# A routed feed-forward kernel: tiles of one expert instead of two, projections made once per token and gathered

## What is computed

```
g = base_g + x @ gate_A[e] @ gate_B[e] * 0.25     # gate_A: 256 x 64, gate_B: 64 x 896
u = base_u + x @ up_A[e]   @ up_B[e]   * 0.25
h = silu(g) * u                                    # 896 wide
oe = h @ base_down + h @ down_A[e] @ down_B[e] * 0.25
out = out + routing[e] * oe                        # routing: softmax of the two bids
```

## Time and profile before

| | |
|---|---|
| median of three runs | 350.17 us (349.76 to 350.34) |
| span of the profiled execution | 343.0 us (the page gives no other time of it) |
| TensorE matmul busy | 262.8 us, 77% |
| VectorE (DVE) busy | 220.6 us, 64% |
| ScalarE (ACT) busy | 160.7 us, 47% |
| GpSimd (POOL) busy | 129.1 us, 38% |
| memory traffic | 133 GB/s over the span |

### The profile page before, as it was taken

How to read it: one execution, slowest core, us unless ns; L and a number is a source line. 1 busy time by engine, 2 the same in 40 slices (tenths; PEclk the granted TensorE clock), 3 DMA queues, 4 the chain that set the end, 5 groups by cost and what they waited for, 6 DMA issues and landing times.

```text
span 343.0 us, 5103 instructions
## 1 busy us (share of the span) xinstructions
PE 262.8 (77%) x1500; PEld 229.4 (67%) x1501; DVE 220.6 (64%) x433; ACT 160.7 (47%) x277; POOL 129.1 (38%) x148
## 2 busy tenths in 40 slices
PE   3474363537278899995999999999999999998600
PEld 2251241214167799994999999999999999997500
DVE  2979975798952881006666777777777777775325
ACT  0443875196336363343455555555555555555211
POOL 3528376537441441109233333333333333311121
PEclk9996566555579899998999999999999999999965
DMA  7803333013663646446244444434344444420065
GB/s 259 240 23 80 70 84 84 26 51 107 177 158 134 210 167 267 175 164 214 44 139 139 139 138 133 143 135 141 134 138 142 138 136 138 140 106 15 15 193 190
DMA packets 30189, 45.67 MB, mean 133 GB/s; under 512 B 13976, under 2 KB 25632, under 8 KB 30176
## 3 DMA queue, kind: packets, MB, share of 16 engines
q0 software_dynamic: 4416, 21.50, 18.9%
q1 hardware_dynamic: 20752, 14.03, 14.6%
q10 hardware_dynamic: 5008, 9.98, 7.9%
HBM read 33.57 MB, written 11.93 MB: 133 GB/s over the span
## 4 chain that ended last, share of the span: by engine, by line
PE 65%; DVE 17%; issue 5%; DMA 4%; POOL 3%; ACT 3%; SPq 1%; DVEq 0%; ACTq 0%; POOLq 0%
PE pY L55 8%; PE pY L59 7%; PE pY L57 7%; PE pG L55 5%; PE pT L1395 5%; PE pG L59 4%; PE pG L57 4%; PE pU L57 4%; PE pU L55 4%; PE pU L59 4%; DMA x_resid<-in_x_dram 2%; DVE q L899 2%; DMA yr<-results 1%; DVE q L819 1%; DVE am L821 1%
## 5 line engine op out<-in xcount | busy, mean ns | idle before, releaser
L496 POOL DMA_INDIRECT results<-yb,dest x19 | 19.0, 998 | 91.9 <-DVE yb L1108 91.9
L55 PE MATMUL pY<-Wd_hi,hT_hi 128*128 128x384 f32 x133 | 47.5, 357 | 0.9 <-ACT Wd_lo L694 0.8
L59 PE MATMUL pY<-Wd_hi,hT_lo 128*128 128x384 f32 x133 | 44.7, 336 | 0.0
L57 PE MATMUL pY<-Wd_lo,hT_hi 128*128 128x384 f32 x133 | 44.6, 336 | 0.0
L490 POOL DMA_INDIRECT bin<-base_products,tok x18 | 22.0, 1221 | 24.8 <-PE pU L59 15.2
L704 ACT CAST hT_hi<-pT 128x896 fp32r<-128x896 f32 x19 | 17.2, 907 | 24.1 <-PE pT L1395 24.1
L680 ACT CAST xaT_hi<-pX 128x256 fp32r<-128x256 f32 x19 | 7.1, 373 | 42.5 <-PE pX L1372 42.0
L55 PEld LDWEIGHTS pY<-Wd_hi,hT_hi 128*128 128x128 f32 x133 | 25.0, 188 | 2.3 <-DVE hT_lo L1096 1.0
L57 PEld LDWEIGHTS pY<-Wd_lo,hT_hi 128*128 128x128 f32 x133 | 25.1, 188 | 0.0
L482 POOL DMA_INDIRECT xin<-normed,tok x19 | 18.6, 979 | 16.9 <-PE pX L1358 9.9
L59 PEld LDWEIGHTS pY<-Wd_hi,hT_lo 128*128 128x128 f32 x133 | 25.0, 188 | 0.0
(11 more groups left out here) (260 smaller groups left out, 742.2 us busy)
## 6 DMA issues: line engine op xcount, KB each, us to landing
base_products<-brow ACTq DMA_DIRECT2D x8, 896.0 KB, 3.9
yr<-results SPq DMA_DIRECT2D x8, 256.0 KB, 4.6
raw<-in_L_ffn_gate_B_dram SPq DMA_DIRECT2D x8, 224.0 KB, 2.7
raw<-in_L_ffn_up_B_dram SPq DMA_DIRECT2D x8, 224.0 KB, 2.5
raw<-in_L_ffn_down_A_dram SPq DMA_DIRECT2D x7, 256.0 KB, 3.0
x_resid<-in_x_dram SPq DMA_DIRECT2D x4, 256.0 KB, 4.8
q<-in_fside_BxS2xS_dram ACTq DMA_DIRECT2D x4, 256.0 KB, 5.7
normed<-q ACTq DMA_DIRECT2D x4, 256.0 KB, 2.8
```

Of the source, the lines that this page charges most:

```text
L55: m.matmul(outs[i], hi, whi[i], start=first, stop=False, skip_group_check=True)
L57: m.matmul(outs[i], hi, wlo[i], start=False, stop=False, skip_group_check=True)
L59: ins = m.matmul(outs[i], lo, whi[i], start=False, stop=last, skip_group_check=True)
L496: g.indirect_dma_start(out=yg, out_offset=bass.IndirectOffsetOnAxis(ap=dest[:, j:j + 1], axis=0), in_=yb[:, :], in_offset=None).then_inc(d ...
```

## The change

A group is one expert (`GE = 1`): 8 groups, so at most 23 tiles instead of 19. The projections x @ gate_A and x @ up_A are made ahead of the loop, for every token and all eight experts, scaled by 0.25 and written to a new tensor in memory (`projected`, a row of 128 values for each token and expert); a tile gathers its 128 rows of it instead of rows of x. A gathered row holds 64 values for gate and 64 for up, so after one transpose gate lies on partitions 0 to 63 and up on 64 to 127. The B matrices lie the same way. The expert's B is copied by ACT into a fixed place for each tile (`stage_B`), and its `down_A` one tile ahead (`stage_dA`). No masks are left. Tile 0 gathers its base rows like the others. PSUM has two banks for the result (`pY[2]`), and the transposes of z and of the projections share a bank with half of `h_T`.

```
-GE = 2
+GE = 1
...
+    xa_rows = nc.dram_tensor("projected", [NB * S * E, P], F32, kind="Internal").ap()
...
+        pZ, pX = pT[:, 1, 0:P], pT[:, 1, P:2 * P]
...
             lo(CH_1 - lo_done[0])
+            pool.wait_ge(s_made, 2 * NT)
+            lo(CH_2 - CH_1)
             def gather(j):
-                if j:
-                    pool.wait_ge(s_xT, j)
+                if j >= 2:
+                    pool.wait_ge(s_xzT, j - 1)
+                g.indirect_dma_start(out=xin[:, j % 2, :], out_offset=None, in_=xa_rows, ...
...
             pool.wait_ge(s_plan, 1)
             pool.wait_ge(s_share, 3)
+            pool.wait_ge(s_made, ITEMS)
+            for i in range(3):
+                pool.wait_ge(d_bn[i], 16 * ITEMS // 3)
+            for j in range(2):
+                gather(j)
+                gather_base(j)
+            lo(NCH - CH_2)
+            for j in range(2, PT + 3):
+                if j < PT:
                     gather(j)
                     gather_base(j)
                 if j >= 3:
                     scatter(j - 3)
```

ACT (base products and projections are items; kind 2 is a projection of 1024 columns):

```
+            def item_out(n):
+                t, kind = item(n)
+                act.wait_ge(s_made, n + 1)
...
+                a.activation(row.rearrange("p (a i) -> p a i", a=2), pp[:, :, 0:w], ACT.Copy,
+                             scale=(1.0, 1.0, SCALING)[kind]).then_inc(s_copied, 1)
+                act.wait_ge(s_copied, n + 1)
...
+                a.dma_start(to, row).then_inc(d_bn[n % 3], 16)
...
+            def tile(j, first=False, ahead=2):
+                h_hi(j, 0, first)
+                h_hi(j, 1, first)
+                e = expert(j + 2) if ahead == 2 else None
+                if ahead == 2:
+                    stage_B(j + 2, 0, e)            # waits s_exp: expand(j+1) done
+                if ahead >= 1:
+                    silu(j + 1)
+                xz_hi_copy(j, not first, ahead == 2)  # waits s_xzT: z_T(j-1) and xa_T(j+2) done
+                if ahead == 2:
+                    stage_B(j + 2, 1, e)
+                if ahead >= 1:
+                    e = expert(j + 1)
+                    stage_dA(j + 1, 0, e)           # waits s_down: down_products(j) done
+                    stage_dA(j + 1, 1, e)
```

DVE:

```
+            def tile(j, par, first=False, second=False, ahead=2):
+                if not first:
+                    z_copy(j - 1, 1 - par, second)
+                h_lo(j, 0)
+                h_lo(j, 1)
+                if ahead >= 1:
+                    g_add(j + 1, 1 - par)
+                    u_add(j + 1, 1 - par)
+                if not first:
+                    z_lo(j - 1)
+                if ahead == 2:
+                    xa_lo(j + 2)
+                if ahead >= 1:
+                    h_mul(j + 1)
+                if not first:
+                    y_copy(j - 1, 1 - par, second)
```

PE:

```
+            for t in range(4, NT):
                 base(t)
+            for t in range(NT):
+                products(2 * NT + t)
+            pe.wait_ge(s_copied, ITEMS)
...
+            def expand(j):
+                pe.wait_ge(s_xalo, j + 1)
+                pe.wait_ge(s_WBe, 2 * (j + 1))
...
+                for i in range(2):
+                    cols = slice(i * IH, (i + 1) * IH)
+                    for k, (x_, w_) in enumerate(((xaT_hi, WBe_hi), (xaT_hi, WBe_lo), (xaT_lo, WBe_hi))):
+                        m.matmul(pG[:, i, 0:IH], x_[0:R, :], w_[0:R, cols], start=(k == 0), stop=(k == 2))
+                        ins = m.matmul(pU[:, i, 0:IH], x_[R:P, :], w_[R:P, cols], start=(k == 0), stop=(k == 2))
+                ins.then_inc(s_exp, 1)
...
+            def tile(j, par, first=False, ahead=2):
+                h_T(j, ahead == 0)          # two halves, 4 and 3 transposes
+                if ahead >= 1:
+                    expand(j + 1)
+                down_products(j, par, range(0, 4))
+                pe.wait_ge(s_hlo, 2 * j + 2)
+                if not first:
+                    ins = z_T(j - 1)
+                if ahead == 2:
+                    ins = xa_T(j + 2, par)      # waits d_xin: gather(j+2) landed
+                ins.then_inc(s_xzT, 1)
+                down_products(j, par, range(4, IC))
+                if not first:
+                    down_B_products(j - 1, 1 - par, expert(j - 1))
```

More of the change, by code:

```diff
@@ L657, in _ @@
             a.activation(share[:, 1, :], dif[:, :], ACT.Sigmoid, scale=-1.0).then_inc(s_share, 1)
[L658 removed]
+            for t in range(3, NT):
                 split(3)
@@ L751, in _ @@
+            tile(PT - 1, ahead=0)
+            xz_hi_copy(PT, xa=False)
             for b in range(0, NB, 2):
@@ L1107, in y_copy @@
                     dve.wait_ge(d_y, 16 * j)
-                v.tensor_copy(yb[:, :], pY[:, 0:H]).then_inc(s_yc, 1)
-            def tile(j, slot, back2=True, back3=True, last=False):
-                if back2:
-                    z_lo(j - 2)
-                h_lo(j - 1)
-                if back2:
-                    y_copy(j - 2, not back3)
-                g_add(j, slot)
-                if not last:
-                    x_lo(j + 1)
-                u_add(j, slot)
-                h_mul(j)
-                if not last:
-                    xa_mask(j + 1)
-                    xa_lo(j + 1)
-                z_mask(j - 1, not back2)
@@ L1136, in _ @@
+            xa_lo(0)
+            g_add(0, 0)
+            u_add(0, 0)
             xa_lo(1)
             h_mul(0)
-            tile(1, 1, back2=False)
-            tile(2, 0, back3=False)
-            tile(3, 1)
-            with dve.Fori(4, PT - 2, 2) as j:
+            tile(0, 0, first=True)
+            tile(1, 1, second=True)
+            with dve.Fori(2, PT - 3, 2) as j:
                 tile(j, 0)
                 tile(j + 1, 1)
-            tile(PT - 1, (PT - 1) % 2, last=True)
-            z_lo(PT - 2)
@@ new lines, in h_T @@
+            def h_T(j, last=False):
+                pe.wait_ge(s_h, j + 1)
+                if not (isinstance(j, int) and j == 0):
+                    pe.wait_ge(s_hlo, 2 * j)
+                for half, chunks_ in enumerate((range(0, 4), range(4, IC))):
+                    if half and not last:
+                        pe.wait_ge(s_xalo, j + 2)
+                    if half and not (isinstance(j, int) and j < 2):
+                        pe.wait_ge(s_zlo, j - 1)
+                    for c in chunks_:
+                        ins = m.transpose(pT[:, half, (c % 4) * P:(c % 4 + 1) * P], hbuf[:, c * P:(c + 1) * P], ident[:, :])
+                    ins.then_inc(s_hT, 1)
@@ L1461, in _ @@
-            expand_B(0, 0, (0, 1), e, first=True)
-            project_A(1, group(1))
-            expand_B(0, 1, (0, 1), e, True)
-            xa_T(1)
-            h_T(0, True)
-            tile(1, back2=False)
-            tile(2)
-            tile(3)
-            with pe.Fori(4, PT - 2, 2) as j:
-                tile(j)
-                tile(j + 1)
-            tile(PT - 1, last=True)
-            z_T(PT - 2)
-            down_B_products(PT - 2, group(PT - 2))
-            down_products(PT - 1, range(IC))
@@ L1481 @@
+            xa_T(0, 0).then_inc(s_xzT, 1)
+            expand(0)
+            xa_T(1, 1).then_inc(s_xzT, 1)
+            tile(0, 0, first=True)
+            tile(1, 1)
+            with pe.Fori(2, PT - 3, 2) as j:
+                tile(j, 0)
+                tile(j + 1, 1)
+            tile(PT - 3, 0)
+            tile(PT - 2, 1, ahead=1)
+            tile(PT - 1, 0, ahead=0)
+            z_T(PT - 1).then_inc(s_xzT, 1)
+            down_B_products(PT - 1, 0, expert(PT - 1))
 _INS = ['x', 'fside_BxS2xS2_0', 'ctx_1024', 'g_xattn', 'g_ffn', 'L0_ffn_expert_wealth', 'L0_ffn_conf_W', 'L0_ffn_conf_b',
```

527 lines of the change are left out of this document (205 added, 322 removed).

## The result

The changed kernel takes 368.25 us, median of three runs (366.35 to 369.57), against 350.17: 1.050 times the time before, 95% interval 1.044 to 1.056. It is slower, by 18.1 us where 21.8 were forecast (372). The profiled execution took 366.35 us with a span of 364.6, 21.6 more than the span of before; the forecast had +22.1.

What follows compares the result with a forecast made beforehand. Matmuls on TensorE were taken to bound the old loop. First `h_T` at 187.0, loop 152.5 and end 8.5 give a last scatter at 348.0 against 325.94: span 365.1, plus 7.17, so 372 us; range 355 to 392.

Steps and rivals of the forecast that it cites:

- Ahead of the loop: Before the first tile: projections (22.6 us) and a round trip through memory delay the first `h_T` by 25.7 us, to 187.0.
- a start under 180 breaks the first step: Sign: first `pT` transposes, expected at about 187, starting under 180 would refute the estimate for the stretch before the first tile.
- The loop: From first to last `h_T`: 22 periods of 6.9 us plus 0.7 for the slow clock, 152.5 against 153.95.
- The ring named: In each tile: `y_copy`, scatter, gather, `xa_T`, ACT's copy, two DVE low parts, `h_mul`, next `y_copy`; 6.9 us a period.
- the gather is in time: Rival in the tile: gather lands in under 2.3 us, the chain through `g_add` sets 6.4 a period; 361 us, chance 0.13.
- The aside that register loads of 0.5 each make ACT's share 7.3: In each tile: ACT has 5.3 us of copies and two register loads; at 0.5 each, ACT makes the period 7.3.
- The halves: In `expand`: the two row halves work at the same time, so the twelve matmuls take 1.25 us instead of 2.46.
- The rival: In `expand`: the row halves don't overlap, period 7.7, 17.6 us more in all; 390 us, chance 0.15.
- The clock: In the loop: rival that PE's clock stays at 1.2 GHz, +75 us, 447, chance 0.04; forecast allowed 0.7 at the start.
- The end: After the loop: 8.5 us from the last `h_T` to the last scatter instead of 10.66, then nothing changes.
- The total: Whole kernel: last scatter 22.1 us later, span 365.1, plus 7.17 from span to median, so 372; chance 0.62.
- the last case: In the loop: rival that the DVE chain alone decides, 5.8 us a tile; 348 us, faster than before; chance 0.06.

Runs made afterwards that it cites:

- the experiment (392.9 less 368.25): Changed kernel with the up products reading rows 0 to 63 like the gate products, so both need the same half of the array: 392.91 us, ratio 1.123.
- all eleven: The eleven kernels with the changed layout: the changed kernel itself and ten edited versions of it; ratios to the kernel before from 1.029 to 1.123.
- the two of the old layout: The kernel before the change (350.17 us) and the same kernel with 21 tile slots instead of 19, two of them empty (360.32 us, one run).
- in the next: The kernel with two implied waits less, plus `g_add` made in two halves, the first released after half of `expand`: 360.98 us, ratio 1.040.

## Why the prediction was right

**Ahead of the loop: right to 1.3 us.** 96 products at 0.233 took 22.4 us (forecast 0.235 and 22.6), and the experiment with a third of them shows them on the path. The forecast puts the last base copy at 147.57 (the 148.47 of before, 0.9 earlier for the first tile's moved matmuls) and the first `h_T` at 187.0, 39.4 apart; measured 38.06. Landing of the write 3.1 (3.2), base rows 5.64 (5.6). `h_mul(0)` took 1.49, not 2.0; it overlaps the last of POOL's subtractions by 0.54, and a steady one takes 1.08. The Trainium skill (SBUF — State Buffer, the section on the shared port of DVE and GpSimd) has the two exclude each other; these 0.4 us agree with it, but no run separates them from another cause. `g_add(0)` and `u_add(0)`, which read one operand from PSUM, took 1.09 and 1.08 beside those subtractions, as in a steady tile. The first `h_T` came at 180.4 and not at 187.0 mostly because the last base copy came 5.2 earlier than forecast: 4.0 of it is the scatter of the first base product's start, 1.2 is base products that ran closer than forecast. So the sign "a start under 180 breaks the first step" was a poor one: it was missed by 0.4 only, for a reason that has nothing to do with the step.

**The loop: right in sum, by a ring that is one of three.** 155.7 against 152.5. The ring named is there and measures 7.08. The forecast's terms for it add up to 6.96 (0.70, 1.31, 2.8, then 0.35, 0.4, 0.2, 0.2, 1.0); it went on with 6.9, which is 1.3 us over 22 periods. The landing was 0.24 shorter than assumed, the steps from `xa_T` to the next `y_copy` 0.37 longer. In 10 of 21 tiles it is the gather that the weight load of `xa_T` waits for; in the others nothing is named. The step that failed is the term of the rival "the gather is in time", 6.4 a period. Counted from the end of `h_mul` in the kernel with the earlier gather, `g_add` starts at +2.9 (forecast +2.5), ACT's copy at +5.0 (+4.6), and the next `h_mul` ends at +7.1 (+6.4): each hand-over was 0.1 to 0.2 short, and ACT was taken as free while it runs the silu. Had it been 6.4, an earlier gather would have brought 11 us by the forecast's 6.9, and 15 from the measured 7.08; it brought 1.7. So naming one ring gave the right period partly by luck, since the one beside it was as long. The aside that register loads of 0.5 each make ACT's share 7.3 isn't the sum of its terms (5.3 + 1.0 = 6.3); ACT is busy for 5.0 us a tile.

**The halves: right.** The rival cost 24.7 us in the experiment (392.9 less 368.25) where the prediction had 17.6 more. 3.6 of the loop's 23.6 us are the first period at the low clock, which the rival left out; for the steady tile it had 0.8 and 0.9 was measured. The Trainium skill (TensorEngine Tiling (Array Packing), Key Properties) says that tiles load and multiply in parallel and that a change of mode drains the array. Pairs 0.01 apart agree with the first. For the second: the first product on half the rows holds the next one off for 0.31 instead of 0.20, and the first full one comes 0.29 after the last of them, so 0.2 a tile if all of that is the drain; no run shows that it is.

**The clock: right.** Behind the base products it fell in the idle stretch (0.59) and was back within the first period (0.75 from 180.4 to 188.4), which was 0.9 longer (0.7); in the loop it is 1.00.

**The end: 3.0 us too low.** Last `h_T` to last scatter 9.76 instead of 8.5 (9.7 to 9.9 in all eleven): the last `y_copy` waits 1.56 for the landing of the scatter before it, since `yb` is one buffer and the last two tiles now lie 3.2 apart. Then 18.8 instead of 17.1 to the end. The code there is the same in all kernels, and that stretch was 17.9 to 19.1 in the eleven and 17.1 and 18.0 in the two of the old layout, so most of these 1.7 can be scatter; 0.6 goes with the longer landing of the read of the results (5.2 after, 4.6 before).

**The total.** The span came within 0.5 us of the forecast's 365.1 by misses that cancel: the first `h_T` 6.6 early, most of it scatter, the loop 3.2 longer, the end 3.0 longer. That closeness is luck; that the kernel gets slower, and that the stretch ahead of the loop is what makes it so, is not. The median is 3.75 below the 372 because the offset from span to median, 7.17, was taken from before, where the profiled execution was a short one: in the runs beside the experiments before's time lies 2.1 above its own span, after's 1.75, and after's median 3.65 above the span of its profile. The chances of the last case don't add up (0.05 and 0.02 of a case that was given 0.06); nothing hangs on it.

## What to carry to other kernels

Work moved ahead of a loop is paid in full where the engine is full, and its round trip through memory is paid on top where the loop can't start without it: here 25 us, against 1.5 us won per tile on tiles of which there are four more. When the engine that was the bound is relieved, write down every ring of hand-overs in the new tile, not only the first one found: here the period fell by 0.16 us at most when one of the first two was cut, or both. And compare distances between the same two events when a stretch ahead of them varies.

## What was not expected of the hardware

- Products on the two row halves start together even when three for one half are issued before three for the other (254.42 and 254.43): the halves work off the instructions on their own, and the period is the same as with alternating issue (6.99 against 7.08).
- ACT's copy of a transpose started some 0.5, 1.2 or 1.9 us after it, the last mostly with no releaser on this core. With two implied waits less it was 1.1 at most in one kernel, and in the next 1.9 again in a third of the tiles.
- After 7.45 us without a matmul PE ran the twelve half-row products at 0.37 a pair instead of 0.20 (clock 0.59 over the stretch); kept busy with products that nobody reads, it ran most of them at 0.20.
